# One DMA turns x2's halves; own orders for the first and last batches; unread products in TensorE's early gaps

## The reference

```
n   = layernorm(x)
A   = softmax((n * w_lhs) @ (n * w_rhs).T) @ n          # 512 x 512 scores
x1  = x + layernorm(A)
x2  = layernorm(x1)
h   = silu((x2 @ w1.T) * s1) * ((x2 @ w2.T) * s2)        # 128 -> 512, twice
h   = gelu((h @ h1.T) * sh1)                             # 512 -> 512
h   = gelu((h @ h2.T) * sh2)                             # 512 -> 512
y   = (h @ w3.T) * s3                                    # 512 -> 128
out = x1 + layernorm(y)
```

## Time and profile before

| | us |
|---|---|
| median of 3 executions | 520.17 (519.22 to 520.48) |
| the profiled execution | 520.69 |
| its span, first to last instruction | 518.9 |
| TensorE busy | 469.5 |
| ScalarE busy | 405.8 |
| VectorE busy | 366.9 |
| GpSimd busy | 314.0 |
| mean granted TensorE clock | 0.975 |

### The profile page before, as it was taken

One profiled execution on the slowest core, in us unless ns is written; L12 is line 12 of the kernel. 1 busy time (PEld: TensorE's weight loads), 2 busy tenths in 40 slices (PEclk: granted clock), 3 DMA queues, 4 the chain that ended last, 5 costly groups with the idle time before them and its releaser, 6 DMA issues.

```text
span 518.9 us, 8118 instructions
## 1 busy us (share of the span) xinstructions
PE 469.5 (90%) x2626; PEld 350.3 (68%) x2626; DVE 366.9 (71%) x1144; ACT 405.8 (78%) x715; POOL 314.0 (61%) x332
## 2 busy tenths in 40 slices
PE   0557599999999999999999999999999999989892
PEld 0355368686868777786868686777778686858571
DVE  3558695977777796969787777869695868654422
ACT  3343398979899898979898998989797989886871
POOL 4313409376684939395866849393958666575464
PEclk9977799999999999999999999999999999999997
DMA  8000000001010000101010100001000000000001
GB/s 302 2 1 23 21 1 1 21 1 40 3 42 0 22 21 0 42 1 42 1 42 2 40 1 22 20 2 42 1 21 0 22 3 20 1 20 2 21 1 40
DMA packets 5659, 11.83 MB, mean 23 GB/s; under 512 B 752, under 2 KB 752, under 8 KB 5616
## 3 DMA queue, kind: packets, MB, share of 16 engines
q1 hardware_dynamic: 5616, 11.28, 6.4%
HBM read 7.09 MB, written 4.19 MB: 22 GB/s over the span
## 4 chain that ended last, share of the span: by engine, by line
PE 83%; ACT 6%; DVE 5%; POOL 2%; issue 2%; DMA 1%; POOLq 0%; SPq 0%; ACTq 0%; DVEq 0%
PE hid_bank L290 46%; PE score_bank L222 8%; PE hid_bank L222 8%; PE score_bank L227 4%; PE score_bank L290 4%; PE score_bank L244 3%; PE score_bank L257 3%; PE score_bank L259 3%; PE score_bank L258 3%; DVE hA L1031 2%; ACT L803 1%; DVE row_max L992 1%; DMA columns<-columns_dram 1%; DVE max_diag L996 1%; ACT gate L764 1%
## 5 line engine op out<-in xcount | busy, mean ns | idle before, releaser
L290 PE MATMUL hid_bank<-hA_hi,w_hi 128*128 128x512 f32 x256 | 108.7, 425 | 1.4 <-DVE hA L1031 1.4
L1367 POOL TENSOR_TENSOR hB_lo<-hB,hB_hi 128x512 fp32r<-128x512 f32 x64 | 81.0, 1289 | 45.5 <-ACT hB_hi L775 45.4
L290 PE MATMUL hid_bank<-hB_hi,w_hi 128*128 128x512 f32 x256 | 101.5, 396 | 0.0
L290 PE MATMUL hid_bank<-hB_lo,w_hi 128*128 128x512 f32 x256 | 101.5, 396 | 0.0
L290 PE MATMUL hid_bank<-hA_lo,w_hi 128*128 128x512 f32 x256 | 101.2, 395 | 0.0
L1372 POOL TENSOR_TENSOR hC_lo<-hC,hC_hi 128x512 fp32r<-128x512 f32 x64 | 80.7, 1284 | 7.1 <-ACT hC_hi L775 7.1
L774 ACT ACTIVATE hC<-hid_bank,columns 128x512 f32<-128x512 f32 x64 | 44.5, 696 | 31.4 <-PE hid_bank L290 31.4
L1333 POOL TENSOR_SCALAR ln_y_var_eps<-ln_y_mean_var 128x4 f32<-128x4 f32 x16 | 3.5, 217 | 102.2 <-DVE ln_y_mean_var L959 102.2
L1031 DVE SCALAR_TENSOR_TENSOR hA<-hid_bank,columns,gate 128x512 f32<-128x512 f32 x64 | 47.6, 747 | 22.2 <-ACT gate L764 22.2
L803 ACT ACT_TABLE_LOAD x47 | 60.3, 1283 | 1.5 <-PEq L1532 0.7
L290 PEld LDWEIGHTS hid_bank<-hA_hi,w_hi 128*128 128x128 f32 x256 | 48.3, 189 | 13.1 <-DVE hA L1031 3.2
(11 more groups left out here) (85 smaller groups left out, 1150.1 us busy)
## 6 DMA issues: line engine op xcount, KB each, us to landing
x_in<-x_dram SPq DMA_DIRECT2D x16, 256.0 KB, 2.6
out_dram<-y_out SPq DMA_DIRECT2D x16, 256.0 KB, 2.0
w_raw<-weights_dram SPq DMA_DIRECT2D x5, 512.0 KB, 6.0
w_raw<-weights_dram SPq DMA_DIRECT2D x1, 256.0 KB, 5.1
columns<-columns_dram SPq DMA_DIRECT2D x1, 9.5 KB, 4.5
```

The costliest lines, as they stand in the source:

```text
L290: mm = nc.tensor.matmul(bank[:, :], lhs, rhs, start=(k == order[0] and n == 0), stop=(k == order[-1] and n == len(pairs) - 1))
L1367: nc.gpsimd.tensor_tensor(hB_lo[:, m, :], hB[:, m, :], hB_hi[:, m, :].bitcast(f32), ALU.subtract).then_inc(hB_lo_ready[m], 1)
```

## The change

Four things are changed.

1. **x2 is split first and turned afterwards, by DMA.** ScalarE rounds `x2n` in SBUF to float16 (`high_x2`), VectorE subtracts (`low_x2`), both write one tile `x2_split`, and SyncE issues one transposing DMA for both halves, eight blocks of 128x128 of two-byte numbers, into `x2T`, which has two buffers. TensorE's `gated` waits for that DMA. `turn_x2` leaves TensorE's list.
2. **y is centred straight into the store buffer** (`y_out`), and GpSimd adds x1 in place; the wait for the earlier store moves from GpSimd to VectorE.
3. **The lists are written anew.** The repeated step has another order, and batches 0 to 2 and the last ones have orders of their own on all engines (`orders`, `BLOCKS[b]`, `ORDER1[b]` and so on). Weight parts arrive in the order 0, 4, 5, columns, x(0), 2, x(1), x(2), 1, 3. The gelus' low halves are still on GpSimd.
4. **TensorE runs products whose result nobody reads** (`keep_warm`), 115 in all, in the first two batches and before the third one's scores.

```diff
-        x2T_hi, x2T_lo = (sb(n, [P, S], f16) for n in ("x2T_hi", "x2T_lo"))
+        x2_split = sb("x2_split", [P, 2, S], f16)
+        x2T = sb("x2T", [P, TWO, 2, T, P], f16)
...
-        y_n = sb("y_n", [P, T, D], f32)
...
@@ SyncE @@
+            def turn_x2(b):
+                sp.wait_ge(x2_lo_ready, b + 1)
+                after(sp, gated_mm[GATED_ORDER[b - 2][-1]], b - 1)
+                sp.dma_start_transpose(x2T[:, b % TWO, :, :, :].rearrange("p h t s -> p (h t) s"),
+                                       x2_split[:, :, :].rearrange("p h s -> p (h s)")).then_inc(
+                                           x2T_landed[b % TWO], 16)
...
@@ SyncE @@
             def step(i):
                 load_x(i)
-                store(i - 6)
+                turn_x2(i - 4)
+                store(i - 7)
...
@@ TensorE @@
+            def keep_warm(count):
+
+                for n in range(count):
+                    nc.tensor.matmul(hid_bank[3][:, :], minus_ones[:, :], hC_lo[:, 0, :], start=True, stop=True)
...
@@ TensorE @@
-            def turn_x2(b):
-                pe.wait_ge(x2n_ready, b + 1)
-                turn(x2T_bank, x2n[:, :, :], x2T_turned)
...
-                if m == GATED_ORDER[0]:
-                    pe.wait_ge(x2T_lo_ready, b + 1)
+                if m == GATED_ORDER[b][0]:
+                    pe.wait_ge(x2T_landed[b % TWO], 16 * (b // TWO) + 16)
+                hi, lo = (x2T[:, b % TWO, half, :, :].rearrange("p t s -> p (t s)") for half in range(2))
...
@@ TensorE @@
             def start():
+                keep_warm(51)
                 turn_x(0)
+                keep_warm(10)
                 scores(0, 3)
...
+                keep_warm(5)
                 shift(0, 3)
...
+                keep_warm(9)
                 pe.wait_ge(exp_done[0], 1)
                 pe.wait_ge(exp_done[1], 1)
                 attend(0, 3)
...
                 turn_x(1)
+                keep_warm(13)
...
+                gather_low()
+                keep_warm(5)
+                shift(1, 3)
...
+                keep_warm(9)
...
+                turn_x(2)
...
+                    keep_warm(13)
                     scores(2, 3)
...
@@ ScalarE @@
-            def high_x2T(b):
-                act.wait_ge(x2T_turned, b + 1)
-                after(act, gated_mm[3], b)
-                nc.scalar.copy(x2T_hi[:, :], x2T_bank[:, :]).then_inc(x2T_hi_ready, 1)
+            def high_x2(b):
+                act.wait_ge(x2n_ready, b + 1)
+                after(act, x2T_landed[(b - 1) % TWO], 16 * ((b + 1) // TWO))
+                nc.scalar.copy(x2_split[:, 0, :], flat(x2n)).then_inc(x2_hi_ready, 1)
...
@@ VectorE @@
-            def low_x2T(b):
-                dve.wait_ge(x2T_hi_ready, b + 1)
-                minus(x2T_lo[:, :], x2T_bank[:, :], x2T_hi[:, :]).then_inc(x2T_lo_ready, 1)
+            def low_x2(b):
+                dve.wait_ge(x2_hi_ready, b + 1)
+                minus(x2_split[:, 1, :], flat(x2n), x2_split[:, 0, :]).then_inc(x2_lo_ready, 1)
...
@@ VectorE, normalize_y @@
-                after(dve, y_ready, b)
-                centred(ln_y, b, lambda t: y_bank[:, t * P:(t + 1) * P], y_n[:, :, :], y_n_ready)
+                after(dve, out_stored[b % TWO], 16 * (b // TWO))
+                centred(ln_y, b, lambda t: y_bank[:, t * P:(t + 1) * P], y_out[:, b % TWO, :, :], y_n_ready)
...
@@ GpSimd, add_ffn @@
-                after(pool, out_stored[b % TWO], 16 * (b // TWO))
-                nc.gpsimd.tensor_tensor(y_out[:, b % TWO, :, :], y_n[:, :, :], x1[:, b % XB, :, :],
+                nc.gpsimd.tensor_tensor(y_out[:, b % TWO, :, :], y_out[:, b % TWO, :, :], x1[:, b % XB, :, :],
...
+            nc.gpsimd.memset(hC_lo[:, 0, :].bitcast(f32), 1.0).then_inc(minus_ready, 1)
```

More of the change, by code:

```diff
@@ L204, in _ @@
             start()
-            for i in range(6, N):
+            for i in range(10, N):
                 step(i)
@@ L304, in layer2 @@
                 pe.wait_ge(hB_lo_ready[k], b + 1)
-                layer(hid_bank[m], k, ORDER2[m], products(general, H2 + k * H + m * P, hB_hi[:, k, :], hB_lo[:, k, :]), h2_mm[m])
+                layer(hid_bank[m], k, ORDER2[b][m], products(general, H2 + k * H + m * P, hB_hi[:, k, :], hB_lo[:, k, :]), h2_mm[m])
             def layer3(general, b, k):
@@ new lines, in ramp @@
+                    layer3(general, 2, 2)
+                    pe.wait_ge(gated_done[1], 4)
+                    gated(general, 3, 3)
+                    pe.wait_ge(yT_ready, 3)
+                    scores(5, 2)
+                    pe.wait_ge(gated_done[2], 4)
+                    layer1(general, 3, 0, 0)
+                    layer1(general, 3, 0, 1)
+                    pe.wait_ge(gated_done[2], 4)
+                    layer1(general, 3, 1, 0)
+                    shift(5, 3)
+                    shift(5, 1)
@@ L714, in main @@
                 ramp()
-                for i in range(4, N):
+                for i in range(6, N - 3):
                     step(i)
@@ L847, in start @@
                 silu(0, 2)
[L849 to L864 removed]
+                high_A(0, 1)
@@ new lines, in start @@
+                silu(0, 3)
+                high_A(0, 2)
+                fetch_exp()
+                softmax(2, 3)
+                high_A(0, 3)
+                softmax(2, 2)
+                softmax(2, 0)
+                softmax(2, 1)
+                fetch_gelu()
+                gelu1(0, 0)
+                gelu1(0, 1)
+                gelu1(0, 3)
+                scale_eps(2)
+                gelu1(0, 2)
+                high_aT(3)
+                high_x2(1)
+                high_xT(3)
@@ new lines, in start @@
+                gelu2(0, 1)
+                gelu2(0, 3)
+                gelu2(0, 0)
+                gelu2(0, 2)
+                fetch_silu()
+                silu(1, 0)
+                silu(1, 1)
+                high_A(1, 0)
+                high_A(1, 1)
+                silu(1, 2)
+                scale_y(0)
+                silu(1, 3)
+                high_A(1, 2)
+                fetch_exp()
+                softmax(3, 3)
+                high_A(1, 3)
+                softmax(3, 0)
+                softmax(3, 1)
@@ new lines, in start @@
+                softmax(3, 2)
+                fetch_gelu()
+                gelu1(1, 0)
+                gelu1(1, 1)
+                gelu1(1, 3)
+                scale_eps(3)
+                gelu1(1, 2)
+                high_aT(4)
+                high_xT(4)
+                high_x2(2)
+                gelu2(1, 1)
+                gelu2(1, 3)
+                gelu2(1, 0)
+                gelu2(1, 2)
+                fetch_silu()
+                silu(2, 0)
+                silu(2, 1)
+                high_A(2, 0)
@@ new lines, in start @@
+                high_A(2, 1)
+                silu(2, 2)
+                scale_y(1)
+                silu(2, 3)
+                high_A(2, 2)
+                fetch_exp()
+                softmax(4, 3)
+                softmax(4, 0)
+                high_A(2, 3)
+                softmax(4, 1)
+                softmax(4, 2)
+                fetch_gelu()
+                gelu1(2, 0)
+                gelu1(2, 1)
+                gelu1(2, 3)
+                gelu1(2, 2)
+                scale_eps(4)
@@ L941, in _ @@
             start()
-            for i in range(3, N):
+            for i in range(5, N - 3):
                 step(i)
@@ new lines, in start @@
+                aggregate(ln_att, 2)
+                low_aT(3)
+                low_xT(3)
+                low_x2(1)
+                normalize_att(2)
+                find_max(3, 0)
+                find_max(3, 3)
+                x1_statistics(2)
+                gated(1, 0)
+                gated(1, 1)
+                aggregate(ln_x1, 2)
+                find_max(3, 1)
+                low_A(1, 1)
+                spread_max(3, 3)
+                low_A(1, 0)
+                gated(1, 2)
+                spread_max(3, 1)
@@ L1324, in _ @@
             start()
-            for i in range(6, N):
+            for i in range(8, N - 3):
                 step(i)
@@ L1503, in _ @@
             start()
-            for i in range(5, N):
+            for i in range(7, N - 2):
                 step(i)
```

1489 lines of the change are left out of this document (1076 added, 413 removed).

## The result

| | us |
|---|---|
| median before, measured beside it | 520.33 (519.22 to 520.88) |
| median after | 503.34 (501.52 to 503.89) |
| ratio after / before | 0.967 (95% interval 0.9641 to 0.9699) |
| the profiled execution after | 503.13 (before 520.69) |
| its span | 501.1 (before 518.9) |

Case A of the forecast came true; the median is 2.1 us above the forecast one. The page of the changed kernel, busy times, clock and DMA, stands against the earlier trace rows. The rows shorten names: `x_split` is the tile `x2_split`, and `x2T<-x_split` is the turn by DMA.

The account below looks back on a forecast made before the run. TensorE was taken to bound the steady part. Gains of 5.6 (eleven periods), 11.6 (early) and 3.3 (tail) sum to 20.5 us, less 1.5 for small waits: profiled execution 501.7, median 501.2 us, range 496 to 520.

Parts of the forecast that it names:

- Case A: The forecast itself: the DMA lands within 6.4 us and fillers warm the clock; 58%, own range 496 to 508 us.
- The turn leaves TensorE, one cut of attend less: Steady period: 0.44 us from the turn and 0.07 from attend, 28.44 to 27.93 us; 5.6 us over eleven periods.
- The DMA hides: Turn of x2 ahead of gated: landing taken as 4.5 us, bounds 2.0 and 7.9, within 6.4 us, costing nothing.
- No difference from reading SBUF: ScalarE's copy (0.58 us) and VectorE's subtraction (0.69 us) for x2 keep their times; 0.1 us either way sits in slack.
- The fillers end at 16.7 us: First 51 unread products, 12 cold and 39 warm, end at 16.7 us; turn of x(0) 0.8 us later, batch 0 gains 5.0.
- From 52.67 to 62.11, +1.5, and to 108.19, +1.5: Early stages: earlier scores and first gated product gain 1.5 us, then shorter periods and vanished waits gain another 1.5 us.
- rival D: Early batches: the clock is not kept or fillers are in the way; 505 to 514 us, 9%.
- The tail, 3.3 us: From 421.05 us on: 0.9 first, 0.95 in each of two batches, 0.5 in the last; 3.3 us gained.
- 1.5 us for small waits: Whole kernel: 1.5 us taken off the summed gain because new orders by hand leave small waits.
- y straight into the store buffer, 0: Store of y: one wait moves from GpSimd to VectorE, on a store issued a period before; cost 0.
- C: Gated products wait for a slow DMA landing and nothing absorbs it; slower than before, 524 or 559 us, 14%.
- B: DMA turn lands a little late, 6.5 to 7.5 us; 512 us, range 503 to 519, 14%.

Follow-up runs that it names:

- e12: Changed kernel with four 128x128 transposes on TensorE ahead of block 0 of the scores of batches 2 to 15: 509.42 us, ratio 0.9799.
- e8: Changed kernel with 4 instead of 13 unread products behind TensorE's branch: 501.06 us, ratio 0.9645.
- e10: Changed kernel with 8 unread products ahead of the branch and 4 behind it, instead of 13 behind it: 500.57 us, ratio 0.9617.
- e11: Changed kernel with 46 instead of 51 unread products ahead of the turn of x(0), 4 instead of 13 behind the branch: 500.0 us, ratio 0.9612.
- e2: Changed kernel without the 13 unread products behind the branch, ahead of scores(2); the other 102 stay: 501.62 us, ratio 0.9665.
- e4: Changed kernel with the DMA turn of x2 issued three times in a row, TensorE waiting for the third: 597.8 us, ratio 1.1543.
- e3: Changed kernel with the DMA turn of x2 issued twice in a row, TensorE waiting for the second: 517.12 us, ratio 0.9965.
- e6: Kernel before with x2 turned by DMA and y centred into the store buffer, old TensorE order, no unread products: 550.02 us, ratio 1.0582.
- e9: As e6, on the kernel before, with the inputs of the DMA turn formed earlier on VectorE and GpSimd: 528.82 us, ratio 1.0161.
- e5: Changed kernel with TensorE's branch moved up behind scores(1) and the 5 unread products there removed: 501.73 us, ratio 0.9652.

## Why the prediction was right, point by point

**The turn leaves TensorE, one cut of attend less: 0.51 us a batch, period 27.93.** Right: 27.93. e12 prices the turn by itself at 0.46 (0.44 taken). The eleven periods gave 5.2 us once the mark is corrected (5.6 foretold); the 0.4 lie in the two steps from 351.83 to 408.12, of which 0.20 is a wait for a late low half of GpSimd at 355.43. The first period is long (28.45) only by the pair of products in which its marks differ.

**The DMA hides.** Right, and by a wide margin in the repeated step: issued 3.8 us behind the end of attend (3.4 foretold), landed 3.1 later, wanted 5.9 after the issue (6.4 foretold). By the Trainium skill (DMA: Bandwidth & Descriptors, "Latency and other measured facts") the estimate was 1.0 us beside the fixed 1.8, that is 2.8; the trace is near it with 3.1. The Trainium skill (VectorE: DVE Perf Modes, "The three transpose paths") has 1309 ns for one 128x128 block by DMA; eight of them in a row, an estimated 10.5 us, are not what this case shows: all eight land in 3.1 us. The budget was not the same everywhere: 3.8 us in batch 1 (issue 77.56, gated 81.40) and 4.5 in batch 14 (439.11, 443.59), where 4.6 was foretold. In batch 1 the margin was 0.8 us, so the 4.5 us that I took for the landing would have cost time there.

**No difference from reading SBUF.** Wrong in size, harmless here: VectorE's subtraction took 1.38 us (median) instead of 0.69, in slack. It is part of why the issue came at 3.8 and not 3.4.

**The fillers end at 16.7 us.** Right: 16.6. Batch 0 gained 5.2 us less the 0.6 of the later turn, 4.6 (5.0 foretold); batch 1 2.7 (3.6 foretold; where the 0.9 went I did not trace). Attend(0) ends at 30.5 and attend(1) at 45.3 (30 and 44 foretold).

**From 52.67 to 62.11, +1.5, and to 108.19, +1.5.** The first of these steps failed: 9.44 us became 9.13, 0.3 instead of 1.5. The second held: 46.08 became 45.47, and with the mark 0.94 later that is 1.5. I placed scores at +4.3 behind the turn of x(2); they came at +7.7, and the first gated product at 54.5 instead of 52. I had summed the 13 products as 3 us of a wait, and had not read that the branch stands ahead of them in the list: TensorE stands still for 2.7 us, the clock falls, and the products then take 4.4 us and end 3.6 us after the inputs of scores (49.48). That is the second half of rival D, at its place, and D's "no pause is left longer than 2 us" was wrong. The trace of the kernel before had the price of the branch, first below; there queued products covered most of it, and the profile puts the 1.3 us of standstill down to VectorE's maxima. The changed kernel's stands behind it (durations in ns, starts in us):

```profile
L724 PEldq COMPARE_BRANCH  x1: 3741/3741/3741, 40.7 to 40.7; - x1
L1130 PEldq COMPARE_BRANCH  x1: 3495/3495/3495, 45.1 to 45.1; - x1
```

e8, e10 and e11 give 2.0 to 2.1 us back, and e2 shows that leaving all 13 out does not. Early part: 9.2 us for 11.6.

**The tail, 3.3 us.** 3.5 measured. The mechanism I named for the waits was half of it: of the waits in the tail before, 2.0 us ended on VectorE's low half of the turned x2 (two of 1.0), which are gone, and 1.4 on hA, of which 1.0 is left.

**1.5 us for small waits.** The parts fell 2.7 us short of their sum (batch 0 0.4, batch 1 0.9, the ramp 1.2, the periods 0.4, less the tail's 0.2), and the 1.5 covered over half of that. It was meant for small waits in the new orders, not for a hole of 2.7 us and a slow clock, so that the total came within 2.1 us owes something to luck.

**y straight into the store buffer, 0.** Right: no wait in the changed trace ends on a store.

**The rivals.** C's mechanism is real: e4 is slower than before at a landing of 9.2 us. Its price was too low, though. By my formula, 12 (9.2 - 6.4) + 2 (9.2 - 6.0) = 40 us; e4 took 87 more in its span: 65 of waits, as the budgets were shorter than taken, and 22 mostly of the clock behind them, as far as the estimate at e4 goes. B's mechanism held in e3, and its price was too low in the same way: a landing of 6.1 us, inside the 6.4 taken, cost 13.8. The case that I had not seen is the one of e6 and e9: the turn by DMA in the old order is slower by 2 to 6%, because VectorE's work for x2 and for the attention meet behind the end of attend.

## What to carry to other kernels

Work taken off the bounding engine counts in full only while everything that it used to hide stays early enough: read, at its old place, who waits next and with what slack, and move those first. A fill of an idle stretch must be laid out against the list that surrounds it: a branch or a late input ahead of it shifts it onto the path. A wait on the bounding engine has two prices, its length while it is short, and, when it is long, sometimes the slower clock behind it (3.3 us cost 3.4 or 5.1 in e4), so a transfer near its budget is a larger risk than its overshoot.

## What the runs showed of the hardware

- **The hole of the branch.** The branch lasts 3.4 to 3.8 us on TensorE's sequencer in all fourteen traces, the kernel before too. The engine stands still for 2.7 to 3.0 of them where little is queued ahead (e3, e4, e5, e8, e11, e12, the changed kernel), and for 1.55 where eight long products were queued (e10). In each trace a 16 KB packet of instruction loads (queue q8) begins 1.0 us into the branch; that the branch waits for it is likely and was not tried.
- **The clock over such a hole.** It was at 0.50 behind holes of 2.73, 2.79 and 2.94 us, and stayed at 1.00 behind 2.70 in e8, 1.55 in e10 and 2.99 in e4, the longest of these. So the length of the hole does not tell by itself. Behind it TensorE worked about 3 us (48.7 to 51.5 in the changed kernel) before the clock was back, and 6 us in e2 (49.98 to 56), where it paused again at 52.9. In the head it rose after 7 to 14 products of the lower level, so the same list starts its first batch up to 1.5 us apart (15.56 in e8, 17.02 in e3).
- **A turn beside an instruction load is slower.** The twelve kernels with the turn by DMA hold 240 turns. In twelve of these a 16 KB packet of instruction loads (queue q8) begins while the turn is under way, and they land after 3.63 to 4.89 us; none of the others takes more than 3.68, and the median is 3.1. Nine of the twelve are first turns, issued while the branch still lasts; the other three stand in the middle of the kernel. The first turns of e5, e6 and e9, where the branch lies earlier, have no such packet and land after 3.16 to 3.18 us, so it is not being the first that slows a turn. No run moves the packet by itself. The first turn of the changed kernel (48.24 to 52.47 us) and, behind it, that of e5 (50.08 to 53.26 us, which shows no row of q8):

```profile
q8 instruction: 1, 0.02, 1.9%
...
x2T<-x_split SPq DMA_TRANSPOSE x1, 4.2
...
x2T<-x_split SPq DMA_TRANSPOSE x1, 3.2
```

- **VectorE and GpSimd at once.** The subtraction for x2 takes 0.66 to 0.69 us where none of GpSimd's low halves runs at its start and 1.30 to 1.39 where one has about 0.8 us left to run, and GpSimd's smallest operation, 0.197 us in the median, takes 1.75 beside VectorE's subtractions:

```profile
239.61 1.29 POOL L2088 TENSOR_TENSOR hB_lo<-hB,hB_hi 128x512 fp32r<-128x512 f32 x1
241.19 1.30 POOL L2088 TENSOR_TENSOR hB_lo<-hB,hB_hi 128x512 fp32r<-128x512 f32 x1 [0.28 <-ACT hB_hi L1181]
...
241.65 1.38 DVE L1495 TENSOR_TENSOR x_split<-x2n,x_split 128x512 f16<-128x512 f32 x1 [0.75 <-ACT x_split L1166]
...
343.38 0.67 DVE L1495 TENSOR_TENSOR e_lo<-exps,e_hi 128x512 f16<-128x512 f32 x1
343.56 1.75 POOL L2054 TENSOR_SCALAR ln_x_var_eps<-ln_x_mean_var 128x4 f32<-128x4 f32 x1 [6.44 <-DVE ln_x_mean_var L1505]
343.95 0.69 DVE L1583 TENSOR_TENSOR hA_lo<-hA,hA_hi 128x512 fp32r<-128x512 f32 x1
```

The Trainium skill (GPSIMD Engine Reference, "1. Specifications") says that GpSimd shares its way into SBUF with VectorE and that the two contend where VectorE reads two operands there; the rows agree in kind. Two runs come close to isolating it: in e6 the subtraction starts beside GpSimd's low halves of the second gelu and takes 1.30 us in 13 of 16 batches, and in e9, where it stands earlier, 0.66 to 0.69 in all 16. In the kernel before the same subtraction read PSUM and took 0.69 us.
